# Sorted message rows padded to one node block per group of 512, in a two-layer graph network on one Trainium2 core

## The reference, cut to what matters

```python
z = jnp.concatenate([node_feats[src], node_feats[dst], edge_feats], axis=1)
z = z @ W.T + b
mean = jnp.mean(z, axis=0)
var = jnp.mean(jnp.square(z - mean), axis=0)
z = (z - mean) * jax.lax.rsqrt(var + BN_EPS) * gamma + beta
msg = jax.nn.sigmoid(z[:, :H]) * jax.nn.softplus(z[:, H:])
agg = jnp.zeros_like(node_feats).at[src].add(msg)
return node_feats + agg
```

## Time and profile before

| what | busy us | share of the span |
|---|---|---|
| PE matmul | 3037.7 | 64% |
| POOL | 2539.8 | 53% |
| DVE | 1924.3 | 40% |
| ACT | 1412.4 | 30% |
| DMA, mean of 16 engines | | 135 GB/s over the span |

### The profile page before, as it was taken

One profiled execution on the slowest core, in us unless ns is written; L12 is line 12 of the kernel. 1 busy time (PEld: TensorE's weight loads), 2 busy tenths in 40 slices (PEclk: granted clock), 3 DMA queues, 4 the chain that ended last, 5 costly groups with the idle time before them and its releaser, 6 DMA issues.

```text
span 4764.4 us, 74664 instructions
## 1 busy us (share of the span) xinstructions
PE 3037.7 (64%) x16593; PEld 2074.8 (44%) x16717; DVE 1924.3 (40%) x4127; ACT 1412.4 (30%) x2638; POOL 2539.8 (53%) x2543
## 2 busy tenths in 40 slices
PE   1777677757878886788888888862121235555366
PEld 1455455544555554455555555531111124444255
DVE  6444444454444456422222222333232334454355
ACT  3222222220000001321121221227677754454500
POOL 4455554544655551466666666547777764454600
PEclk9787787768887887899999999985555557777599
DMA  3222222222222221577777777754444444545343
GB/s 96 72 63 78 75 74 64 90 68 78 87 84 85 84 83 32 182 231 232 239 229 234 230 228 233 226 190 147 135 140 135 146 132 134 162 139 168 106 100 102
DMA packets 360456, 645.05 MB, mean 135 GB/s; under 512 B 62184, under 2 KB 226380, under 8 KB 355216
## 3 DMA queue, kind: packets, MB, share of 16 engines
q1 hardware_dynamic: 264016, 392.92, 26.0%
q0 software_dynamic: 93440, 218.82, 15.5%
q10 hardware_dynamic: 2880, 32.11, 1.9%
HBM read 439.34 MB, written 204.28 MB: 135 GB/s over the span
## 4 chain that ended last, share of the span: by engine, by line
PE 37%; issue 19%; another core or an unknown queue 14%; ACT 10%; DVE 9%; DVEq 8%; DMA 2%; ACTq 0%; SPq 0%; POOL 0%; POOLq 0%
PE PS L1644 6%; PE PS L1489 6%; PE PS L1638 5%; PE PS L1629 5%; PE PS L1479 5%; PE PS L1661 4%; ACT arena L940 2%; DMA Q<-z_tab 2%; DVEq L383 2%; DVEq L1069 1%; PE PS L1475 1%; ACT Q L935 1%; DVEq L1360 1%; PE PS L1550 1%
## 5 line engine op out<-in xcount | busy, mean ns | idle before, releaser
L725 POOL DMA_INDIRECT Q<-h_tab,src_i x960 | 943.8, 983 | 804.8 <-PE PS L1556 361.6
L752 POOL DMA_INDIRECT m_tab<-Q,pos_i x784 | 834.1, 1064 | 492.8 <-ACT Q L959 265.8
L725 POOL DMA_INDIRECT arena<-p_tab,src_i x784 | 743.6, 949 | 617.7 <-issue 213.8
L1671 PE MATMUL PS<-ident,arena 128*128 128x128 f32 x784 | 203.5, 410 | 808.6 <-DVE arena L1386 426.6
L1489 PE MATMUL PS<-Q 128*128 x2684 | 490.2, 337 | 178.1 <-DVE Q L1071 81.8
L1302 DVE BATCH_NORM_STATS2 stats<-arena 128x512 f32 (+1 forms) x392 | 251.5, 684 | 712.3 <-ACT arena L920 688.2
L1489 PEld LDWEIGHTS PS<-Q 128*128 128x128 f32 x2684 | 419.8, 237 | 272.6 <-issue 268.3
L920 ACT ACTIVATE arena<-PS,LB 128x512 f32<-128x512 f32 x392 | 243.2, 686 | 993.1 <-remote 859.9
L1671 PEld LDWEIGHTS PS<-ident,arena 128*128 128x128 f32 x784 | 131.2, 205 | 869.3 <-issue 714.9
L1661 PE MATMUL PS<-Q 128*128 x2336 | 400.5, 328 | 154.2 <-issue 77.2
L1661 PEld LDWEIGHTS PS<-Q 128*128 128x128 f32 x2336 | 349.4, 230 | 209.3 <-issue 207.1
(11 more groups left out here) (219 smaller groups left out, 4026.9 us busy)
## 6 DMA issues: line engine op xcount, KB each, us to landing
z_tab<-arena SPq DMA_DIRECT2D x196, 512.0 KB
Q<-z_tab SPq DMA_DIRECT2D x196, 512.0 KB
Q<-m_tab SPq DMA_DIRECT2D x196, 264.0 KB
arena<-in_edge_t SPq DMA_DIRECT2D x196, 256.0 KB
arena<-dst_tab SPq DMA_DIRECT2D x196, 128.0 KB
count_tab<-Q SPq DMA_DIRECT2D x11, 1568.0 KB
Q<-count_tab ACTq DMA_DIRECT2D x10, 1568.0 KB
arena<-count_tab ACTq DMA_DIRECT2D x10, 1568.0 KB
```

What stands on the lines that cost most here:

```text
L725: nc.gpsimd.indirect_dma_start(buf[:, s * GT + k, 0:width], None, table, bass.IndirectOffsetOnAxis(src_i[:, t:t + 1], 0)).then_inc(landed[ ...
L752: nc.gpsimd.indirect_dma_start(m_tab, bass.IndirectOffsetOnAxis(pos_i[:, t:t + 1], 0), mrow[:, s, k, :], None).then_inc(ms.scattered[s], 16)
L1671: ins = turn(PS[:, 2 + q, t * P:(t + 1) * P], msg_t[:, q, t * P:(t + 1) * P], ident[:])
```

## The change

- **Padding.** In each batch every block's rows are padded up to a multiple of 512, so that a group of 512 places has rows of one block only. The batches get room for FIRST = 112 + 48 = 160 and LAST = 84 + 48 = 132 groups, SG = 292 in all, and all 292 are always read. `words2` holds one block number per group.
- **Zeros.** Places that no edge takes must hold zeros, so SP writes the whole of `m_tab` with zeros beforehand: nine groups after each of the 20 table stores in C0, two groups in each of the 48 passes of its loop in C1, 16 more after that loop, before the last load from `base_tab`. ACT, SP and POOL wait for it at three later points.
- **Sums.** No inner loop and no running counter: buffers are static. The one-hot is a `tensor_tensor` (`src_f` keeps only the low part of the node number). DVE loads the block number into a register ahead of each add. The small counting matmul goes; refills wait for `sg.sum_ready`.
- **Buffers and order.** MR = 10 row buffers, refilled five steps later instead of three; 20 sorted groups for each eight.
- **zin comes free earlier.** The sigmoid goes to a buffer `gate` of its own and `scale_z` to `core` (both in the space of `H`); SP reloads `zin` after `scale_z` instead of after `message`.

```diff
-    MR = 7
+    MR = 10
-    OFF = [0, 2, 4, 6, 7, 9, 11, 13, PER]
-    LAST = NG - FIRST
+    OFF = [0, 3, 5, 8, 10, 13, 15, 18, PER]
+    FIRST, LAST = ((k1 - k0) * BG + NT - 1 for k0, k1 in BATCH)
+    SG = FIRST + LAST
+    ZG0, ZG1, REST = 9, 2, 16
...
+            def zero_rows(g, n):
+                sp.dma_start(m_tab[ds(g * GE, n * GE), :].rearrange("(g p k) e -> p g (k e)", p=P, k=GT), rep(zeros, n)
+                             ).then_inc(sg.rows_zeroed, 16)
...
                              ).then_inc(dn.moved[par], 16)
+                zero_rows(entry * ZG0, ZG0)
...
                 load_base(i * 2 + 2)
+                zero_rows(i * ZG1 + (ITEMS + 1) * ZG0, ZG1)
+            zero_rows(SG - REST, REST)
             sp.wait_ge(srt.ranked, JOBS - 1)
             load_base(JOBS - 1)
...
-                    if not (isinstance(j, int) and j + MR >= FIRST):
-                        sp.wait_ge(sg.summed, j + 1)
-                        load_sorted(j + MR, q)
+                    if not (isinstance(k, int) and k * PER + o + MR >= FIRST):
+                        sp.wait_ge(sg.sum_ready, k * PER + (o + 1))
+                        load_sorted(k * PER + (o + MR), o % MR)
...
-                    sp.wait_ge(ms.msg_t_ready, g + 1)
+                    sp.wait_ge(ms.dve_step, g + 1)
                     sp.dma_start(zin[:, s, :], square(z_tab, g)).then_inc(ms.z_in[s], 16)
-                at = back8(d, s, 3)
+                at = back8(d, s, 5)
...
-                nc.scalar.activation(zin[:, s, 0:GE], zin[:, s, 0:GE], ACT.Sigmoid, bias=bn[:, 10:11], scale=bn[:, 8:9])
+                act.wait_ge(ms.msg_t_ready, group_of(d, s) + 1)
+                nc.scalar.activation(gate[:, s, :], zin[:, s, 0:GE], ACT.Sigmoid, bias=bn[:, 10:11], scale=bn[:, 8:9])
...
+            def add_sum(n, o):
+                dve.wait_ge(sg.sum_ready, n + 1)
+                dve.wait_ge(sg.sum_added, n + SD)
+                nc.vector.reg_load(at_window, words2[0:1, ds(n, 1)])
+                w = window(dve.snap(at_window))
+                a = MSUM[:, ds(w, 1), :].rearrange("p a b -> p (a b)")
+                v.tensor_tensor(a, a, PS[:, SD + o % SD, 0:F], ALU.add).then_inc(sg.sum_added, 1)
+            def sum_sorted(k, o, base=0):
+                j = k * PER + (base + o)
+                dve.wait_ge(sg.row_in[o % MR], (k * 2 + (base + o) // MR) * 16 + 16)
+                src = mrow_in[o % MR][:, :, F:F + 1].rearrange("p a b -> p (a b)")
+                v.tensor_tensor(shot[:, o % SD, :].rearrange("p (a b) -> p a b", b=P), bc(src, P), rep(iota[:], GT),
+                                ALU.is_equal).then_inc(sg.hot_ready, 1)
+                if not (isinstance(j, int) and j < SD - 1):
+                    add_sum(k * PER + (base + o - SD + 1), (o + 1) % SD)
...
+                pe.wait_ge(sg.hot_ready, j + 1)
+                pe.wait_ge(sg.sum_added, j + 1)
+                for t in range(GT):
+                    ins = mm(PS[:, SD + o % SD, 0:F], mrow_in[o % MR][:, t, 0:F], shot[:, o % SD, t * P:(t + 1) * P],
+                             start=t == 0, stop=t == GT - 1)
+                ins.then_inc(sg.sum_ready, 1)
```

More of the change, by code:

```diff
@@ L208, in build_gnn @@
         part_tmp, _ = carve(arena, NT * (F + 1), 2, 9 * F)
+        zeros, _ = carve(arena, ARENA - GT * MW, GT * MW)
         src_low, b = carve(q_space, b, DT)
@@ L246, in build_gnn @@
         mrow, a = carve(q_space, a, RZ, GT, MW)
-        mrow_in, a = carve(q_space, a, MR, GT, MW)
+        mrow_q, a = carve(q_space, a, MR - 2, GT, MW)
+        mrow_s, _ = carve(stats_flat, 0, 2, GT, MW)
+        mrow_in = [mrow_q[:, q] for q in range(MR - 2)] + [mrow_s[:, q] for q in range(2)]
         shot, a = carve(q_space, a, SD, GE)
@@ L452, in sorted_of @@
                 return []
-            return [(k * PER + o, o % MR, k * 2 + o // MR) for o in range(OFF[s], OFF[s + 1])]
+            return [(k, o) for o in range(OFF[s], OFF[s + 1])]
         def in_conv(eng, slot, extra):
@@ L712, in _ @@
             nc.gpsimd.memset(ones_bf[:], 1.0)
+            nc.gpsimd.memset(zeros, 0.0)
             nc.gpsimd.memset(AGG, 0.0).then_inc(agg_zeroed, 1)
@@ L884, in _ @@
                     squares(1)
+            act.wait_ge(sg.rows_zeroed, 16 * (ITEMS + NT + 1))
             def turned_h(i):
@@ L1099, in sort_tables @@
                     step(v.tensor_reduce(total[0:NT, 0, b:b + 1], hist[0:NT, k0 * KB:k1 * KB], AX.X, ALU.add))
+                step(v.tensor_scalar(total_n[0:NT, 0, :], total[0:NT, 0, :], GE - 1.0, None, ALU.add))
+                step(v.tensor_scalar(total_n[0:NT, 1, :], total_n[0:NT, 0, :], 9, None, ALU.logical_shift_right))
+                step(v.tensor_scalar(total[0:NT, 0, :], total_n[0:NT, 1, :], float(GE), None, ALU.mult))
                 for b in range(NBT):
@@ L1355, in sum_sorted @@
[L1355 to L1366 removed]
+            at_window = dve.alloc_register("dve_window3")
@@ L1647, in _, with sum_sorted @@
                     ins.then_inc(p1.done, 1)
-            pair = pe.alloc_register("pe_pair3")
-            pe.reg_mov(pair, 0)
-            def sum_sorted(j, q):
-                lo, hi = windows(pe, j, words2)
-                with pe.Fori(lo, hi):
-                    m = tick(pe, pair)
-                    pe.wait_ge(sg.hot_ready, m)
-                    pe.wait_ge(sg.sum_added, m)
-                    for t in range(GT):
-                        hot = shot[:, ds(m % SD, 1), t * P:(t + 1) * P].rearrange("p a e -> p (a e)")
-                        ins = mm(PS[:, ds(m % SD + SD, 1), 0:F].rearrange("p a b -> p (a b)"), mrow_in[:, q, t, 0:F],
-                                 hot, start=t == 0, stop=t == GT - 1)
-                    ins.then_inc(sg.sum_ready, 1)
-                mm(PS[:, 0, 0:1], ones_bf[:], ones_bf[:, 0:1], start=True, stop=True).then_inc(sg.summed, 1)
+            def sum_sorted(k, o, base=0):
+                j = k * PER + (base + o)
+                pe.wait_ge(sg.hot_ready, j + 1)
[4 more added lines that the diff above has]
+                ins.then_inc(sg.sum_ready, 1)
             def turn_msg(d, s):
@@ L1678, in pass2 @@
                 if back8(d, s, 0):
-                    for j, q, u in sorted_of(d, s):
-                        sum_sorted(j, q)
+                    for k, o in sorted_of(d, s):
+                        sum_sorted(k, o)
             pe.wait_ge(norm.ready, 1)
@@ L1684, in _ @@
             in_eights(pe, 2, pass2)
-            with pe.Fori(0, LAST // MR) as t:
-                for q in range(MR):
-                    sum_sorted(t * MR + (FIRST + q), q)
-            for k in range(SD - 2):
-                tick(pe, pair)
-            pe.wait_ge(sg.sum_added, pe.snap(tick(pe, pair) + 1))
+            with pe.Fori(0, LAST // PER) as t:
+                for o in range(PER):
+                    sum_sorted(t, o, FIRST)
+            for o in range(LAST % PER):
+                sum_sorted(LAST // PER, o, FIRST)
+            pe.wait_ge(sg.sum_added, SG + SD)
             for i in range(NI):
```

140 lines of the change are left out of this document (60 added, 80 removed).

## The result

The changed kernel takes 4617.3 us (median of 4; 4615.2 to 4622.4) beside 4761.5 for the kernel before on the same chip, ratio 0.970 with a 95% interval of 0.9688 to 0.9713. The profiled execution took 4618.0 us with a span of 4616.2. The forecast of 4550 us was 67 us too low; the range held the time.

The account below looks back on a forecast made before the run. No one engine throughout: POOL bounds M1 and M3, a ring of POOL, ACT, z loads and DVE M2, DVE's instruction stream E. Span 4764.4 - 158 - 71 + 19 = 4554, plus 2.0, less 6.6: 4550 us; range 4455 to 4650.

Parts of the forecast that it names:

- C0 and C1: The two node-product stages, where zeros are written: 19 us more, bounds 0 and 60.
- the gathers hide it: In C0 and C1: POOL's gathers run ahead and cover the zeros' DMA time, 151 and 81 us.
- The one place that I had put on the path: End of C1: zeros queued ahead of the last base row stall PE 4 to 10 us, taken as 8.
- M1: Pass 2 from first scatter to first sorted one-hot, bound by POOL: no change, at most 32 us won.
- M3: Last scatters of pass 2, bound by POOL, 105 us before: no change.
- M2: Pass 2 where messages and sorted sums run together: 533 us falls to 375, 158 less; bounds 59 and 192 less.
- two more steps of slack: In M2: z loads stand behind older refills, so ACT's 172 us wait mostly goes and POOL becomes the limit.
- M2 stays a ring: Rival: DMA at 0.85 to 0.9 keeps z and refills late; M2 450 instead of 375, total 4625; chance 0.17.
- the rival with 1.165 us and 403: In M2: scatters slow as DVE gets busier, to 1.165 us each, M2 403 instead of 375; no chance given.
- E: Sums alone after the last scatter, 132 pairs, bound by DVE's instruction stream: 229 us falls to 158, 71 less.
- PE's 1.15 us: In E: PE's shown time for a pair, taken as the limit after the change, 132 x 1.15.
- The DMA's 1.09 us: In E: DMA time for a row group at 248 GB/s, from 99 GB/s at 0.40 of the engines.

Follow-up runs that it names:

- e1: Changed kernel without zero writes in C0 and C1: first batch's go out in one go before M1, second's in pieces during M1; 4702.9 us, ratio 0.9852.
- e10: Changed kernel with z loaded only once the message of eight groups before is made, and half of each refill's bytes in E; 4545.9 us.
- e2: Changed kernel with refills seven steps behind the sums instead of five; ratio 0.9557.
- e3: Changed kernel with PE multiplying only two of the four tiles of a sorted row group, half of each sum left out; ratio 0.9574.
- e5: Changed kernel with DVE's register load before each add done twice; ratio 0.9631.
- e9: Changed kernel with added PE matmuls in M2, two after each sum and three per step, into an unread bank; ratio 0.9649.
- e6: Changed kernel with the second batch's zero writes moved from C0 and C1 into M1; ratio 0.9677.
- e7: Changed kernel with refills seven steps behind and only half the sum matmuls, together; ratio 0.9547.
- e11: The changed kernel again, word for word, on another chip; 4534.5 us, ratio 0.964.

## Why the prediction was right in sign and 67 us off

- **C0 and C1** (forecast 19, measured 46.6; the zero writes', e1). The step that failed is "the gathers hide it": I read the 362 us that POOL waits for PE as cover, and looked for the cost only in transfers that come late. The one place that I had put on the path is there, and gone in e1. PE's timeline in the changed kernel:

```profile
1869.35 0.49 PE L1567 MATMUL PS<-Q,upper_bf 128*128 128x392 bf16 x1 [5.22 <-DMA Q<-base_tab]
```

  5.2 us for a forecast of 8 (4 to 10). The rest shows as waits for DVE's table tiles, not for gathers.
- **M1** (0; measured -3): right. **M3**: POOL's, as forecast; by the windows it holds 64 scatters in 88 us now, where it held 73 in 105.
- **M2** (forecast 158 less, measured 81 with M3). The step that failed is "two more steps of slack [...] So the 172 us wait should mostly go". The wait was 166.6 us. Releasing z early bought 7 us at most (e10), since the load still stands in SP's queue behind refills, and a refill waits for a sum. What it is worth once the queue is in order, no run shows. At a lag of five steps the refill of step s stands ahead of the z load of step s+6; two steps more (e2) left 4 us of the wait and gave 59 us. I had named this as the rival "M2 stays a ring" at 450 us, with the DMA engines as its driver; it came out at 466, over the 430 that I had set as the mark of a wrong forecast, and its driver is not the one I named: M2's DMA share was 0.66, not 0.85 to 0.9, and half the matmuls (e3), with all the bytes in place, gave as much as the queue. That the bytes have no part at all is not shown: no run takes them out of M2.
- **POOL next to denser DVE work.** A scatter takes 1055 ns, 1064 before: the rival with 1.165 us and 403 falls. In the twelve runs above it lies between 1053 and 1069. The Trainium skill ("SBUF — State Buffer", section "Who interferes with whom"), by whose rule such one-hots cost POOL nothing, agrees with these traces, though the one-hot before had two inputs in SBUF too. M2 did not become POOL's all the same: POOL waits 115.6 us there for ACT.
- **E** (forecast 71 less, measured 104.5). The mechanism is right: DVE's gaps went, the register load is hidden (e5). Too large were two terms. PE's 1.15 us was its pace while it waited for DVE; now it keeps up with 0.88 and has room (e3). The DMA's 1.09 us came of dividing a mean rate by a mean share; the stage moved 300 GB/s, 0.90 us a group. So the limit is DVE's 0.87, which I had worked out as 0.9 and put below the two others. The DMA's 0.90 lies 4% from it, so that halving PE's work (128.0) or the DMA's (126.3) changes next to nothing: 5.3 us to the first one-hot, 131 x 0.91, 3.2 at the end.
- **Sum.** 28 us of zeros and 77 us of M2 too little were partly paid by 33 of E and 10 in P1 and M1: 62 us of span. The other 5 are the profiled execution: I set it 6.6 us above the median, as before the change, and it lay 0.7 above. That the total came within 1.5% is in part such luck: E's error hides a third of the other two.

## What to carry to other kernels

A queue served in order passes a wait from one user to the other: when a release is moved earlier, check what else stands ahead of the instruction in its queue, and what that waits for; here the lag of a neighbour (five or seven steps) was worth 59 us on the chip with the longest M2, and the early release no more than the 7 us by which like runs differ. Waits of two engines for each other are one ring, and cures of its links do not add up; a wait that vanishes from the profile can come back at another line (e9). Bytes that no engine waits for can still cost: 79 MB in two stages with a DMA share of 0.25 cost 47 us on one chip and 60 on another, found only by taking them out. And compare a stage only with a run on the same chip that has it unchanged.

## What was not expected of the hardware

- A sum can be seen by two other engines 4 to 8 us after PE's records of its matmuls end, and a turned message by a third after 8; around the one shown above the granted clock is 1.0 and DVE and ACT are idle (4147 to 4149 us). Half the matmuls shorten the adds' waits in M2 and M3 (77 us for 119 in e6), though not beside seven steps (e7: 91, for 89 in e5); writing the loop out does (73 for 89), filling PE up to a clock of 0.87 does not (88), and a fifth buffer does, but not the total. The waits also depend on the chip (e11). Their cause stays open.
- The same kernel takes 553 or 514 us for M2 and M3 on two chips, though the instructions take the same time; C0, C1 and the stretch with P1 differ as well, and the ratio to the kernel before moved with them, 0.970 and 0.964.
- 43 MB of zeros written at once, with nothing beside them but set-up, cost 111 us, 388 GB/s (e1).
